# Query and key stacks of an attention kernel by DMA transpose instead of TensorE transpose

## The reference, cut to what matters

```python
xn = _rms_norm(x, g_norm) * (1.0 + scale) + shift
q, k, v = split(xn @ W_qkv)                       # 16 heads of 64
q = _rms_norm(q, g_q); k = _rms_norm(k, g_k)
attn = softmax(einsum('bhqd,bhkd->bhqk', q, k) * d ** -0.5)
o = einsum('bhqk,bhkd->bhqd', attn, v)
x = x + (o + o @ W_out)
x = x + causal_depthwise_conv(x) + b
```

## Time and profile before

| what | value |
|---|---|
| median of three executions | 2490.99 us |
| the profiled execution, its own time | 2491.03 us |
| its span in the trace | 2489.2 us |
| granted TensorE clock, mean of the span | 0.985 of full |
| PE, DVE, ACT, POOL busy | 95%, 84%, 73%, 26% of the span |
| DMA queue of SP, packet time as a share of 16 engines | 91.6% |
| HBM read and written | 137.20 MB, 56.66 MB |

### The profile page before, as it was taken

How to read it: one execution, slowest core, us unless ns; L and a number is a source line. 1 busy time by engine, 2 the same in 40 slices (tenths; PEclk the granted TensorE clock), 3 DMA queues, 4 the chain that set the end, 5 groups by cost and what they waited for, 6 DMA issues and landing times.

```text
span 2489.2 us, 54244 instructions
## 1 busy us (share of the span) xinstructions
PE 2370.1 (95%) x20794; PEld 1527.7 (61%) x20794; DVE 2091.5 (84%) x3371; ACT 1827.0 (73%) x2836; POOL 641.6 (26%) x451
## 2 busy tenths in 40 slices
PE   6689999899899999999999999999999999999899
PEld 1445555555466666666666666666666666666688
DVE  6867988888878888888888888888888888888876
ACT  4566878888777778777777787877777777777732
POOL 1122333232332222323322233223212222221100
PEclk9799999999999999999999999999999999999999
DMA  8899999999999999999999989999988988889971
GB/s 364 237 244 235 193 180 191 184 186 229 195 200 178 198 195 194 188 194 227 201 213 182 212 181 200 187 183 225 211 173 170 181 171 163 170 166 172 180 187 52
DMA packets 1234657, 484.99 MB, mean 195 GB/s; under 512 B 1139552, under 2 KB 1197792, under 8 KB 1231968
## 3 DMA queue, kind: packets, MB, share of 16 engines
q1 hardware_dynamic: 1234400, 481.53, 91.6%
HBM read 137.20 MB, written 56.66 MB: 78 GB/s over the span
## 4 chain that ended last, share of the span: by engine, by line
PE 62%; DVE 20%; issue 5%; ACT 4%; SPq 3%; DMA 1%; POOL 0%; ACTq 0%; POOLq 0%
PE proj L1029 31%; PE scores L971 10%; DVE neg L1557 9%; PE values L990 9%; PE proj L1054 8%; DVE p_pair L1566 7%; ACT p_pair L1208 3%; SPq L777 2%; DVE bias L1560 2%; PE proj L1059 1%; PE misc L1071 1%; ACT late L1200 1%; DMA w_sb<-w_dram 1%; PE values L1005 1%; PE values L997 1%
## 5 line engine op out<-in xcount | busy, mean ns | idle before, releaser
L1029 PE MATMUL proj<-w_sb,xn_sb 128*128 128x384 f16 x6144 | 1037.2, 328 | 21.9 <-DMA w_sb<-w_dram 15.1
L1200 ACT ACTIVATE late<-scores,bias,l_scale 128x1024 f32<-128x1024 f32 x512 | 615.6, 1203 | 347.3 <-DVE bias L1560 328.0
L1029 PEld LDWEIGHTS proj<-w_sb,xn_sb 128*128 128x128 f16 x6144 | 588.2, 98 | 427.4 <-issue 29.3
L1566 DVE TENSOR_TENSOR p_pair<-late,p_pair 128x1024 f16<-128x1024 f32 x512 | 616.9, 1247 | 126.8 <-ACT p_pair L1208 126.8
L1557 DVE TENSOR_REDUCE neg<-scores 128x1 f32<-128x1024 f32 x512 | 623.5, 1218 | 113.4 <-PE scores L971 110.2
L1208 ACT ACTIVATE p_pair<-late 128x1024 f16<-128x1024 f32 x512 | 511.1, 1050 | 2.6 <-DMA pT<-p_pair 2.6
L990 PE MATMUL values<-pT,v_pair 128*64 128x256 f16 x6144 | 390.3, 277 | 20.5 <-ACT inv_row L1268 14.2
L971 PE MATMUL scores<-late 64*128 64x512 f16 x3072 | 376.4, 378 | 14.4 <-ACT late L1200 12.0
L990 PEld LDWEIGHTS values<-pT,v_pair 128*64 128x64 f16 x6144 | 319.7, 111 | 100.1 <-issue 77.3
L1473 POOL TENSOR_TENSOR rs<-ms,power 128x16 f32<-128x16 f32 x63 | 183.0, 2905 | 406.0 <-DVE ms L1580 405.7
L1054 PE MATMUL proj<-late,wo 128*128 128x256 f16 x2304 | 267.7, 273 | 1.1 <-issue 1.1
(11 more groups left out here) (181 smaller groups left out, 2031.2 us busy)
## 6 DMA issues: line engine op xcount, KB each, us to landing
w_sb<-w_dram SPq DMA_DIRECT2D x121, 384.0 KB, 4.0
o_dram<-oT_pair SPq DMA_DIRECT2D x124, 128.0 KB, 2.5
out<-late SPq DMA_DIRECT2D x54, 256.0 KB, 2.9
x_in<-in_x SPq DMA_DIRECT2D x25, 512.0 KB, 4.5
late<-in_x SPq DMA_DIRECT2D x25, 512.0 KB, 4.0
wq_raw<-in_L_cond_W_qkv SPq DMA_DIRECT2D x8, 1536.0 KB, 11.0
late<-o_dram SPq DMA_DIRECT2D x12, 1024.0 KB, 6.3
xn_dram<-late SPq DMA_DIRECT2D x21, 512.0 KB, 3.3
```

Source lines behind the costliest of these rows:

```text
L1029: last = nc.tensor.matmul(proj[:, t % 2, 0:6 * DH], xn_sb[:, t, i * K + c, :], w_sb[:, c, j, :], start=(c == 0 and i == j == 0), stop=(c = ...
L1200: nc.scalar.activation(prob[:, h, :], scores[:, h, :], ACT.Exp, bias=bias[:, s:s + 1], scale=const["l_scale"][:, 0:1], accum_out=total[:, ...
L1566: nc.vector.tensor_tensor(p_pair[:, s % 4, 1, :], prob[:, h, :], p_pair[:, s % 4, 0, :], ALU.subtract).then_inc(lo_done, 1)
```

## The change

- The four `stacks` on PE of each unit are left out from unit 1's on (those of unit 0, made before the loop, stay), and with them three `read_stacks` on ACT and one `read_keys` on DVE (in output units four on ACT and none on DVE). In their place SP issues two DMA transposes a unit, `transpose_qk(w, parity, hf)`, each of 128 by 2048 f16 from `qk_pair` into one half of `stack`. That of half 0 is in step 5, behind `transpose_p` and ahead of `store_o` and the weight loads; that of half 1 is the first thing in step 7, ahead of `transpose_p`. Each waits for `h_hi` and `h_lo` of its half and for the scores of the unit before.
- `stack` is laid out with its halves apart, so that each transpose writes one run.
- `score` of step 0 waits for both transposes (semaphores `st_in`). `high_halves` waits for the transpose of the other half, which read `qk_pair`, in place of the PE transposes.
- `normalise(w, 1)` is in step 5 behind `low` in all units, and `high_halves(w, 1)` in step 6 ahead of `exponent` in all units. In units 0 to 7 that is a new place for both; in output units it is where they were.
- Waits of `project` and `out_product` on `h_ev`, which guarded the PSUM banks that the transposes used, go, or become waits for the reader of the bank.

The description in words also speaks of stores of the front in halves between tiles. The diff has no line that changes a store.

```diff
-        stack = late[:, 0:8192].rearrange("p (a j n) -> p a j n", a=2, j=4)
+        stack = late[:, 0:8192].rearrange("p (a f j n) -> p a f j n", a=2, f=2, j=4)
...
+            def transpose_qk(w, par, hf):
+                sp.wait_ge(h_hi, 2 * w + hf + 1)
+                sp.wait_ge(h_lo, 2 * w + hf + 1)
+                need(sp, qk_done, NS * (w - 1))
+                sp.dma_start_transpose(stack[:, par, hf].rearrange("p j (t n) -> p (j t) n", n=P),
+                                       qk_pair[:].rearrange("p j a t d -> p (j a t d)")).then_inc(st_in[hf], 16)
...
                 for p in range(K):
+                    if qkv and p == 7:
+                        transpose_qk(w, 1 - par, 1)
                     for h in range(2):
                         if p:
                             transpose_p(u, 2 * p - 2 + h)
                         elif begun:
                             transpose_p(u - 1, NS - 2 + h)
+                    if qkv and p == 5:
+                        transpose_qk(w, 1 - par, 0)
...
             def score(u, p, par):
                 need(pe, exp_done, slot(u, 2 * p))
-                if p == 0:
-                    pe.wait_ge(h_ev, 3 * u + 2)
-                    pe.wait_ge(k_ev, u + 1)
-                if p == KH:
-                    pe.wait_ge(h_ev, 3 * u + 3)
+                if u == 0 and p == 0:
+                    pe.wait_ge(h_ev, 2)
+                    pe.wait_ge(k_ev, 1)
+                elif u == 0 and p == KH:
+                    pe.wait_ge(h_ev, 3)
+                elif p == 0:
+                    for hf in range(2):
+                        pe.wait_ge(st_in[hf], 16 * u)
...
-                        stacks(w, 1, 1, misc[:], (h_ev, 3 * w + 1))
-                        stacks(w, 1, 0, proj[:, 0, :], (y_ev, 2 * T + 1) if outs else
-                               (qkv_ev, K * w + (9 if gives_early(u) else 7)))
...
-                    if qkv and outs and p == 5:
-                        stacks(w, 0, 0, misc[:], (f_ev, 2 * T if fins else 0))
-                        stacks(w, 0, 1, proj[:, 1, :], (qkv_ev, K * w + 8))
...
             def high_halves(w, hf):
                 act.wait_ge(h_n, 2 * (2 * w + hf) + 2)
-                need(act, h_tr, 4 * w + 2 * hf)
+                if w == 0 or (w == 1 and hf == 0):
+                    need(act, h_tr, 4 * w + 2 * hf)
+                else:
+                    act.wait_ge(st_in[1 - hf], 16 * (w - 1 + hf))
...
                         if qkv:
-                            read_stacks(w, 1 - par, 0, 0, 0, misc[:])
-                            read_stacks(w, 1 - par, 0, 1, 1, proj[:, 1, :])
-                        if qkv and outs:
                             high_halves(w, 1)
-                    if qkv and outs and p == 7:
-                        read_stacks(w, 1 - par, 1, 1, 2, misc[:], k_ev)
...
-                    if qkv and not outs and p == 6:
-                        high_halves(w, 1)
...
-                    if qkv and p == 7:
-                        read_stacks(w, 1 - par, 1, 0, 3, proj[:, 0, :])
...
-                    if p == 6 and qkv and not outs:
-                        normalise(w, 1)
...
-                    elif p == 7 and qkv:
-                        read_keys(w, 1 - par)
...
-                    if p == 5 and qkv and outs:
+                    if p == 5 and qkv:
                         normalise(w, 1)
```

More of the change, by code:

```diff
@@ L593, in main @@
         h_ev = sem("h_ev")
+        st_in = [sem(f"st_in{i}") for i in range(2)]
         k_ev = sem("k_ev")
@@ L971, in score @@
                             last = nc.tensor.matmul(scores[:, h, n * HN:(n + 1) * HN],
-                                                    stack[rows_, par, i, p * P:(p + 1) * P],
-                                                    stack[rows_, par, j, n * HN:(n + 1) * HN],
+                                                    stack[rows_, par, p // KH, i, (p % KH) * P:(p % KH + 1) * P],
+                                                    stack[rows_, par, n, j, :],
                                                     start=(i == 0 and j == 2), stop=(i == 1))
@@ L1011, in project @@
                     need(pe, qkv_ev, K * w + t - 1)
[L1012 to L1016, removed]
+                    if w == 1 and t == 0:
+                        pe.wait_ge(h_ev, 3)
                     if fins is not None and t < 2:
@@ L1132, in unit @@
                                  (qkv_ev, K * w + 7) if qkv else (y_ev, 2 * T - 1))
-                        free1 = ((h_ev, 3 * w + 2) if qkv else (y_ev, 2 * T),)
+                        free1 = ((qkv_ev, K * w + 8) if qkv else (y_ev, 2 * T),)
                         if p == 5:
@@ L1142, in unit @@
                                     ((oT_ld, 8 * (T - par) + 16), (last_xr_ld[0], 16), (eye_done, T - par + 2),
-                                     (y_ev, 2 * T) if hh else (h_ev, 3 * U)))
+                                     (y_ev, 2 * T if hh else 2 * T - 1)))
                     elif last:
                         tail_begin((p - 4) // 2, p % 2)
-                    if qkv and outs and p == 5:
-                        stacks(w, 0, 0, misc[:], (f_ev, 2 * T if fins else 0))
-                        stacks(w, 0, 1, proj[:, 1, :], (qkv_ev, K * w + 8))
                     if fins and p == 1:
-                        out_transposes(T - 1, 0, (k_ev, u + 1))
+                        out_transposes(T - 1, 0, (f_ev, 2 * T - 2))
                     if fins and p == 4:
@@ L1156, in unit @@
                         attend(u - 1, 3, 1 - par, 0)
-                    if qkv and not outs and p == 5:
-                        stacks(w, 0, 0, misc[:], (qkv_ev, 0))
-                        stacks(w, 0, 1, proj[:, 1, :], (qkv_ev, K * w + 8))
             keep_clock(36)
@@ L1243, in read_stacks @@
                 act.wait_ge(h_tr, 4 * w + count + 1)
-                nc.scalar.activation(stack[:, par, 2 * j:2 * j + 2, hf * HN:(hf + 1) * HN],
+                nc.scalar.activation(stack[:, par, hf, 2 * j:2 * j + 2, :],
                                      bank.bitcast(F16).rearrange("p (a n) -> p a n", a=2),
@@ L1570, in read_keys @@
                 dve.wait_ge(h_tr, 4 * w + 3)
-                nc.vector.tensor_copy(stack[:, par, 2:4, HN:2 * HN],
+                nc.vector.tensor_copy(stack[:, par, 1, 2:4, :],
                                       misc[:].bitcast(F16).rearrange("p (a n) -> p a n", a=2)).then_inc(k_ev, 1)
```

## The result

| | before | after |
|---|---|---|
| time, median (lowest to highest), us | 2491.91 (2490.4 to 2495.42) | 2567.24 (2565.07 to 2568.37) |
| span of the profiled execution, us | 2489.2 | 2565.3 |
| granted clock, mean of the span | 0.985 | 0.971 |
| first scores 0 to 8 apart, against before | | +27.3 us |
| first scores 8 to 24 apart, against before | | +45.5 us |

The ratio is 1.0299, 95% interval 1.0287 to 1.031: 3% slower, outside the range. They say where the error is: in units 8 to 23, for which the forecast had +4.8 us, and to a smaller part in the first eight.

What follows compares the result with a forecast made beforehand. Output units were taken as PE-bound to step 5, then shared by PE and the loop DVE, ACT, DVE. -3.7 + 15 + 2.1 - 0.2 + 2 + 2.6 + 4.8 = +22.6 on 2491.0: 2513.6 us, range 2495 to 2542.

Steps and rivals of the forecast that it cites:

- PE work of output units: Output units: of the PE work removed in steps 5 and 7, only 0.16 us a unit comes back, 3.7 us gained.
- units 1 to 7: First score waits for half 1's transpose: 2.5 us for each of units 1 to 6, 15 us; unit 7 -0.2.
- unit 0: Unit 0 is bound by its weights: 2.2 - 0.9 + 0.8 = 2.1 us slower.
- clock, early units: Longer PE waits in step 7 cost granted clock: 2 us taken, bounds 0 and 6 x 2.5.
- units 8 to 23, queue: Score waits for half 1 behind `load_x`: 0.2 us in 13 units, 2.6; units 14 and 22 with `load_xn`, 4.8.
- units 24 to 30, queue: Units 24 to 30 have no such loads ahead of half 1's transpose, so no queue cost.
- the order on DVE: Early units: `normalise(w, 1)` between `low` of step 5 and `maximum` of step 6 lengthens the loop by 1.9 us a unit.
- Rival 2: SP's queue: landing is not in order, half 1 lands 4.4 us after issue, the new wait costs nothing; 2501.8 us, chance 0.17.
- SP waits for DVE in steps 5 and 6, and both fit there: Output units: SP's pauses for DVE have room for both transposes, counted at 2.3 us each.
- rival 3: Units 8 to 23 with `load_x`: the queue becomes the bound, 16 x 2.3 = 37 us; 2543 us, chance 0.11.
- the loop DVE, ACT, DVE: Early units: `normalise` in its new place lengthens this loop by 1.9 us a unit, hiding the later weights' 1.3.
- the weights: Early units: four weight loads behind half 0's transpose come 2.2 us later, PE has 0.9 less work: +1.3 us, hidden.

Runs made afterwards that it cites:

- x12: Changed kernel with its two transposes issued in unit 0 only, and `normalise(w, 1)` and `high_halves(w, 1)` of units 0 to 7 in before's places; 2490.45 us, ratio 0.9994.
- x1: Changed kernel with its two DMA transposes issued in unit 0 only, later units scoring with the stacks of units 0 and 1; 2498.97 us, ratio 1.0033.
- x3: Changed kernel with `load_x`, weight quarters 2 and 3 and step 6's `xn` load issued in step 7 behind half 1's transpose; 2528.36 us, ratio 1.0158.
- x13: Before with DMA stacks from unit 9, `load_x` and weights behind half 1, second-half read-out and store later, `xn` loads moved; 2482.57 us, ratio 0.9958.
- x7: Changed kernel with only weight quarter 3 moved, to step 7 right behind half 1's transpose; 2549.56 us, ratio 1.0232.
- x6: Changed kernel with only `load_x` moved, from step 6 to step 7 right behind half 1's transpose; 2564.13 us, ratio 1.0314.

## Why the prediction was wrong

| term | predicted | measured |
|---|---|---|
| PE work of output units | -0.16 each, -3.7 in all | -0.16 each in units 25 and 30 of after; -3.0 in all in x12 |
| units 1 to 7 | +14.8 | +23.8 |
| unit 0 | +2.1 | +3.5 |
| clock, early units | +2 | about +9, inside the line of units 1 to 7 |
| units 8 to 23, queue | +7.4 | +45.5 + 2.6 |
| units 24 to 30, queue | 0 | +3.4 + 1.1 |

**What held.** That PE only seems to set the pace: in x12 PE's busy time fell by 50 us (2370.1 to 2320.2), and 21 of the 23 output units gained 0.11 to 0.19 us each. That the order on DVE costs something in early units: 8.5 us in x1 against x12, where I had 1.9 x 6 = 11.4. That a transfer lands some 2 us behind the one ahead of it: half 1 landed at 1074.58, quarter 2 ahead of it at 1072.6. Rival 2 had nothing for it: in the timelines of before, after and x3 no transpose landed ahead of a transfer issued directly before it.

**The step that failed** is the sentence on output units, "SP waits for DVE in steps 5 and 6, and both fit there". I had priced a transpose by the distance of landings, 2.3 us, and had not measured the pauses into which two of them should go, though the rows were there: 2.8 and 2.4 us, each with loads right in front. The issue of half 0 took 3.19 us and that of half 1, behind two loads, 5.39. So I charged only the last transfer, against loads where they had stood before. They stood 2.3 us later at issue, and half 1 landed 2 us behind *them*. That is the first wait; the second was not in the sum at all, though rival 3 named its condition: quarter 3 over 6 us behind the first score. It was 7.4 behind in unit 18. Rival 3 had the place and the mechanism, at a chance of 0.11. It ended at 2543 because it priced the 16 units at 2.3 us instead of the (45.5 + 2.6) / 16 = 3.0 measured, 11 us in all, and took the early units (8 short) and units 24 to 30 (4.5 short) as forecast.

**"No reserve" was the wrong picture too.** I read the queue as a quantity (41 us of transposes in 71; 91.6% of packet time). x3 moves the same 514 MB with the same number of packets at a busy share of 97.9% and saves 39 us (share times span, the packet time is 2478 us in the changed kernel and 2472 in x3); x13 is at 97.7% and faster than before. The bound is not the queue's total but who stands behind whom in the last 20 us of a unit.

**The early units.** I put the loop DVE, ACT, DVE (+1.9) above the weights (+1.3). The weights won: they were issued 336.62 - 285.12 = 51.5 us into unit 2 against 325.87 - 278.2 = 47.7 in before, 3.8 us later, not 2.2: half 0 alone took 3.27 us to issue, and the slots ahead of it ended about 1 us later in the unit. Behind that wait the clock fell: the projection's 24 matmuls took 5.93, 6.54, 5.74 and 6.83 us in units 1, 2, 5 and 6 against 4.07, and before had only unit 6 at 5.88. I had booked 2 us for it with the bound 15; measured by these rows it is 8.8 - 1.8 = 7 us, and some 2 more in unit 4. Half 1, whose landing I used for the sum, was in time in unit 2: it landed at 352.98, and PE's own work lasted until the score at 353.76.

**Units 24 to 30** have no `load_x`, but PE still waited up to 1.85 us for half 1, and in three of them up to 1.32 us for quarter 3. In unit 27 PE waited 1.62 us for half 1, and 0.3 us of this showed, since the exponent was done at nearly the same time.

## What to carry to other kernels

A transfer put into an in-order queue is priced by how long the queue's issuing engine stays in it and by the length of the pause that it should fill, read from the timeline of that engine between its neighbours; then every transfer behind it is shifted and each consumer checked, not only the new one's. When a change moves work from a busy engine to a queue, order the queue by due time in the same step: the change with its 62 transposes cost 76 us in one order and 38 in another, and with 46 of them, and a copy moved that they had made room for, the kernel was 10 us faster than before. And a freed bank or buffer may be worth more than its freed time: here the 0.49 us per unit came from a copy that could be moved once the bank was no longer shared.

## What the runs showed of the hardware

How long SP stays in the issue of one and the same transpose differs with what stands ahead of it. Over the kernel (issue ns min/median/max; to landing), both halves together, in after and then in x3:

```profile
L785 SPq DMA_TRANSPOSE late<-qk_pair x62: 1823/3266/7123, 193.6 to 2388.0; - x62
DMA to landing us min/median/max: 4.2/5.5/9.2
```

```profile
L785 SPq DMA_TRANSPOSE late<-qk_pair x62: 1868/2456/3612, 194.5 to 2346.1; - x62
DMA to landing us min/median/max: 4.2/4.6/6.8
```

These medians mix two cases, and the timeline of SP parts them. Half 0, in the same place in both kernels, has a median of 2.4 and 2.3 us. Half 1 in the 15 output units with `load_x` has 4.9 us in after and 5.0 in x7, right behind two direct loads; 3.5 in x6, behind one; 2.5 in x3, behind none. To landing, half 1 takes 7.0 us (median of all 31) in after and 4.6 in x3. So each load right ahead went with 1.0 to 1.5 us more in which nothing else of the queue is issued.

A direct load of the same 512 KB takes 0.34 us of issue (`load_x`, above) and 4.8 to land. The Trainium skill ("Advanced Engine Details and Errata", X-Bar Transpose (TRN2)) has transpose DMAs as fast as regular ones; by the landing this is near, by the time in which SP can issue nothing else it is not: 3.3 us against 0.34.

The granted clock is the other thing. A pause of PE of 2 to 4.5 us was followed by 24 matmuls at 5.7 to 6.9 us in most early units, and one of 2.6 us in unit 13 by 2.77 us instead of 1.50, while x7 had pauses of 1.6 to 2.8 us in the same place and no slower matmul in units 10, 12, 13 and 18. The cost of a wait is the wait plus what the clock takes behind it, and the second part came at some places and not at others that look alike.
